# State-space scan on one Trainium2 core: C and B read from a double tile in SBUF, exponent banks in two pairs, instructions 1024 columns wide

## What is computed

```python
dt = jax.nn.softplus(dt_raw + dt_bias)
a = jnp.exp(-jnp.exp(A_log) * dt)
Bh = jnp.repeat(_rms(Braw), HEADS_PER_GROUP, axis=2) + B_bias
Ch = jnp.repeat(_rms(Craw), HEADS_PER_GROUP, axis=2) + C_bias
phi = jnp.cumsum(dt, axis=1)[..., None] * rope_freqs
Bh = _rope(Bh, phi)
Ch = _rope(Ch, phi)
u = xh * dt[..., None]

def step(h, inp):
    a_t, u_t, b_t, c_t = inp
    h = a_t[..., None, None] * h + u_t[..., None] * b_t[:, :, None, :]
    y = jnp.einsum('bhpn,bhn->bhp', h, c_t)
    return (h, y)
```

## Time and profile before

| | us |
|---|---|
| median of 3 runs | 2638.09 |
| lowest and highest | 2632.52 and 2638.44 |
| the profiled execution, its own time | 2641.73 |
| its span, first to last instruction | 2639.7 |
| first product of the scan starts | 203.0 |
| last VectorE multiplication into `M` of the scan starts | 1467.8 |
| VectorE busy between 300 and 1400 us | 96% |

### The profile page before, as it was taken

The page is one execution under the profiler, slowest core; times in us unless marked ns, Lnnn a source line. Parts: engine busy times, 40 slices in busy tenths (PEclk is TensorE's granted clock), DMA queues, the critical chain, the costliest instruction groups (busy, mean ns, idle before and its releaser), DMA issues. The chain is left out here.

```text
span 2639.7 us, 61136 instructions
## 1 busy us (share of the span) xinstructions
PE 2154.0 (82%) x19761; PEld 1590.8 (60%) x19761; DVE 1937.0 (73%) x5279; ACT 1543.8 (58%) x3098; POOL 1486.5 (56%) x2287
## 2 busy tenths in 40 slices
PE   8946888888888888878887799786799767758887
PEld 5634655565655665655655588565355445548887
DVE  4538999999999999999999444466333267747776
ACT  5657898999899999999897122355122112212222
POOL 2447787888788788888787222244111144414444
PEclk9976898988898888998897799888899878879999
DMA  5766666666666666666675367343222233321110
GB/s 171 245 193 175 163 167 174 173 176 174 161 169 180 168 176 175 168 174 175 161 183 142 108 204 233 128 139 124 77 84 84 71 103 116 117 69 37 48 48 28
DMA packets 295374, 373.58 MB, mean 142 GB/s; under 512 B 44852, under 2 KB 234871, under 8 KB 295127
## 3 DMA queue, kind: packets, MB, share of 16 engines
q1 hardware_dynamic: 285254, 343.10, 47.0%
q0 software_dynamic: 9872, 27.28, 3.1%
HBM read 151.03 MB, written 85.00 MB: 89 GB/s over the span
## 5 line engine op out<-in xcount | busy, mean ns | idle before, releaser
L667 POOL TENSOR_TENSOR p_CR<-p_pc 128x256 f32<-128x256 f32 x512 | 373.3, 729 | 189.5 <-DVE p_pc L991 165.9
L671 POOL TENSOR_TENSOR p_BR<-p_pb 128x256 f32<-128x256 f32 x512 | 373.4, 729 | 26.5
L748 PE MATMUL p_ps_sc<-p_CR,p_BR 64*128 64x128 f32 x4096 | 341.6, 313 | 54.8 <-DVE p_M L1004 32.9
L748 PEld LDWEIGHTS p_ps_sc<-p_CR,p_BR 64*128 64x128 f32 x4096 | 289.6, 213 | 113.9 <-issue 86.4
L881 ACT ACTIVATE p_D<-p_ps_x 128x512 f32<-128x512 f32 x512 | 289.5, 593 | 109.5 <-PE p_ps_x L714 108.8
L1004 DVE TENSOR_TENSOR p_M<-p_ps_sc,p_D 128x512 f32<-128x512 f32 x512 | 327.9, 680 | 29.7 <-PE p_ps_sc L748 28.9
L991 DVE SCALAR_TENSOR_TENSOR p_pc<-p_ps_c,p_beta,p_cs 128x256 f32<-128x256 f32 x512 | 243.0, 475 | 46.8 <-DMA p_sn<-p_tr_s 31.3
L763 PE MATMUL p_ps_y<-p_M,p_uexp 128*32 128x128 f32 x4096 | 259.7, 282 | 0.0
L991 DVE SCALAR_TENSOR_TENSOR p_pc<-p_ps_c,p_beta,p_sn 128x256 f32<-128x256 f32 x512 | 242.6, 474 | 0.0
L997 DVE SCALAR_TENSOR_TENSOR p_pb<-p_ps_b,p_beta,p_cs 128x256 f32<-128x256 f32 x512 | 242.5, 474 | 0.0
L997 DVE SCALAR_TENSOR_TENSOR p_pb<-p_ps_b,p_beta,p_sn 128x256 f32<-128x256 f32 x512 | 242.5, 474 | 0.0
(11 more groups left out here) (277 smaller groups left out, 5293.4 us busy)
## 6 DMA issues: line engine op xcount, KB each, us to landing
p_cs<-p_tr_c SPq DMA_DIRECT2D x256, 256.0 KB, 4.1
p_sn<-p_tr_s SPq DMA_DIRECT2D x256, 256.0 KB, 4.5
p_phib<-scratch_phi SPq DMA_DIRECT2D x256, 128.0 KB, 3.1
p_x<-scratch_rt SPq DMA_DIRECT2D x72, 128.0 KB, 2.0
scratch_ro<-p_o POOLq DMA_DIRECT2D x72, 128.0 KB, 2.0
p_xT<-in_xT SPq DMA_DIRECT2D x64, 128.0 KB, 4.6
scratch_u<-p_u SPq DMA_DIRECT2D x16, 512.0 KB, 3.8
scratch_wu<-p_wu SPq DMA_DIRECT2D x16, 512.0 KB, 4.3
```

The costliest lines, as they stand in the source:

```text
L667: e.tensor_tensor(CR[:, p, g, :], pc[:, g % 2, 0, :], pc[:, g % 2, 1, :], ALU.add).then_inc(S["rotC"], 1)
L671: e.tensor_tensor(BR[:, p, g, :], pb[:, g % 2, 0, :], pb[:, g % 2, 1, :], ALU.add).then_inc(S["rotB"], 1)
L748: m = e.matmul(sc_ps[half][:, (g * 2 + b) * L:(g * 2 + b + 1) * L], BR[half * 64:half * 64 + 64, p, 2 * q + g, b * L:(b + 1) * L], CR[half ...
```

## The change

1. `c_ps` and `b_ps` are gone. The tile `bc` in SBUF becomes double (by chunk), and the products read it there. Of the copies into PSUM only the change of sign is left, in place, one ScalarE instruction of 512 columns a chunk (`signed_bc`), one step earlier than `held_bc` was. SyncE's `load_bc` waits for the products of the last chunk but one.
2. The two freed banks make the exponent banks two pairs; the two score banks are now one pair. `exponents` needs one pair free, not both banks.
3. `D`, `M`, the transposes' copies `BT`, the second rounding step of the angles, `magnitude` and `sines` work on twice the columns in half the instructions; of `turned` each half step now has one of eight transposes, where it had two of four, and ScalarE's order is rewritten to that.
4. Four constants of the start are held in tiles that are used later.

The core of the diff:

```diff
-        bc = sb("bc", [P, 4, CT])
+        bc = sb("bc", [P, 2, 4, CT])
...
-        c_ps, b_ps, y_ps, ns_ps = (ps(n) for n in ("c", "b", "y", "ns"))
-        x_ps = [ps(f"x{i}") for i in range(2)]
-        sc_ps = [ps(f"sc{i}") for i in range(2)]
+        y_ps, ns_ps = (ps(n) for n in ("y", "ns"))
+        x_ps = [ps2(f"x{i}") for i in range(2)]
+        sc_ps = ps2("sc")
...
             def load_bc(c):
-                at_least(e, S["bcp_ok"], c, 4, 0)
+                at_least(e, S["prodC"], c, 2 * NG * NB, -2 * NG * NB)
+                at_least(e, S["prodB"], c, 2 * NG * NB, -2 * NG * NB)
...
             def exponents(t, p, q):
-                at_least(e, S["x_ok"], i, 1, 0)
-                bank = [x_ps[(i + half) % 2] for half in range(2)]
+                at_least(e, S["x_ok"], i, 1, -1)
+                bank = [x_ps[i % 2][:, half, :] for half in range(2)]
...
-            def held_bc(c):
+            def signed_bc(c):
                 at_least(e, S["bc_in"], c, 96, 96)
-                for bank, rows, free in ((c_ps, 2, "prodC"), (b_ps, 0, "prodB")):
-                    at_least(e, S[free], c, 2 * NG * NB, 0)
-                    e.activation(bank[:, 0:CT], bc[:, rows, :], ACT.Copy).then_inc(S["bcp_ok"], 1)
-                    e.activation(bank[:, CT:2 * CT], bc[:, rows + 1, :], ACT.Copy, scale=sign[:, :]).then_inc(S["bcp_ok"], 1)
+                e.activation(bc[:, c % 2, 1:4:2, :], bc[:, c % 2, 1:4:2, :], ACT.Copy, scale=sign[:, :]).then_inc(S["bcp_ok"], 1)
...
-                e.activation(D[:, n, :], x_ps[i % 2][:, :], ACT.Exp).then_inc(S["x_ok"], 1)
+                e.activation(D[:, 2 * q:2 * q + 2, :], x_ps[i % 2][:, :, :], ACT.Exp).then_inc(S["x_ok"], 1)
...
-                    e.scalar_tensor_tensor(out=pc[:, g % 2, n - 2, :], in0=c_ps[:, (n - 2) * CT:(n - 1) * CT], scalar=beta[:, k, n, g:g + 1],
+                    e.scalar_tensor_tensor(out=pc[:, g % 2, n - 2, :], in0=bc[:, c % 2, n, :], scalar=beta[:, k, n, g:g + 1],
                                            in1=tr[:, p, g % 2, g // 2, :], op0=ALU.add, op1=ALU.mult).then_inc(S["prodC"], 1)
...
-                    e.scalar_tensor_tensor(out=pb[:, g % 2, n, :], in0=b_ps[:, n * CT:(n + 1) * CT], scalar=beta[:, k, n, g:g + 1],
+                    e.scalar_tensor_tensor(out=pb[:, g % 2, n, :], in0=bc[:, c % 2, n, :], scalar=beta[:, k, n, g:g + 1],
                                            in1=tr[:, p, g % 2, g // 2, :], op0=ALU.add, op1=ALU.mult).then_inc(S["prodB"], 1)
...
-                e.tensor_tensor(M[:, m_slot(p, n), :], sc_ps[n % 2][:, :], D[:, n, :], ALU.mult).then_inc(S["m_ok"], 1)
+                m = m_slot(p, n)
+                e.tensor_tensor(M[:, m:m + 2, :], sc_ps[:, :, :], D[:, n:n + 2, :], ALU.mult).then_inc(S["m_ok"], 2)
```

More of the change, by code:

```diff
@@ L555, in expand @@
                 p = k % 2
-                used, ready = count(e, t, 2 * NG, -2 * NG), count(e, t, 2, 2)
+                used, ready = count(e, t, 2 * NG, -2 * NG), count(e, t, 1, 1)
                 if not (isinstance(t, int) and t < 2):
@@ L568, in load_g @@
                 if t >= 2:
-                    e.wait_ge(S["x_mm"], place["D", t - 2, U - 1] + 1)
+                    e.wait_ge(S["x_mm"], place["D", t - 2, NQ - 1] + 1)
                 for half in range(2):
@@ L787, in new_state @@
             def new_state(t, p):
-                at_least(e, S["x_ok"], place["B", t, NQ - 1], 1, 1)
+                at_least(e, S["x_ok"], place["B", t, 1], 1, 1)
                 at_least(e, wu_got[p], t - p, 8, 16)
@@ L934, in state @@
+                e.activation(BT[:, 2 * h:2 * h + 2, :, :].rearrange("p q a n -> p q (a n)"), x_ps[i % 2][:, :, :], ACT.Copy
+                             ).then_inc(S["x_ok"], 1)
             def state(t):
-                i = place["S", t, 0]
+                i = place["S", t]
                 at_least(e, S["x_mm"], i, 1, 1)
@@ L942, in own, with step @@
                         return bass.AP(tensor=ap.tensor, offset=ap.offset, ap=[list(ap.ap[0]), [2 * P + 16, 2], [32, BATCH * NQ], [1, HD]])
-                    e.activation(own(ST[r, t % NB, 0, 0, h * HD:h * HD + HD]), own(x_ps[i % 2][r, h * HD:h * HD + HD]), ACT.Copy
+                    e.activation(own(ST[r, t % NB, 0, 0, h * HD:h * HD + HD]), own(x_ps[i % 2][r, 0, h * HD:h * HD + HD]), ACT.Copy
                                  ).then_inc(S["x_ok" if h else "kept"], 1)
+            def step(t, k, c):
+                p = k % 2
+                ahead, s3, k3 = t + 3 < T, t + 3, (k + 3) % NB
+                decays(t, 1)
+                if ahead:
+                    in_turns(s3, k3, 0)
+                    near_turns(s3, k3, 0)
+                if t and t <= LAST:
+                    turned(t - 1, 1)
+                if ahead:
+                    in_turns(s3, k3, 1)
+                decays(t, 2)
+                if ahead:
+                    near_turns(s3, k3, 1)
+                    whole_turns(s3, 0)
+                decays(t, 3)
+                if k == 2 and c + 1 < NC:
+                    signed_bc(c + 1)
+                if ahead:
+                    in_turns(s3, k3, 2)
+                    near_turns(s3, k3, 2)
+                if 2 <= t < LAST + 2:
+                    state(t - 2)
+                if t < LAST:
+                    turned(t, 0)
+                if t + 2 < T:
+                    magnitude(t + 2, p)
+                if t + 1 < T:
+                    decays(t + 1, 0)
+                if t + 2 < T:
+                    sines(t + 2, p)
+                if ahead:
+                    in_turns(s3, k3, 3)
+                    near_turns(s3, k3, 3)
+                    whole_turns(s3, 1)
             def all_turns(s):
@@ L952, in _ @@
                 if s == 0:
-                    held_bc(0)
-                for v in range(2):
-                    magnitude(s, s, v)
+                    signed_bc(0)
+                magnitude(s, s)
                 sines(s, s)
-            for n in range(2):
-                decays(0, n)
+            decays(0, 0)
             all_turns(2)
@@ L1010, in new_state @@
                 if t >= NB:
-                    e.wait_ge(S["x_mm"], place["S", t - NB, 0] + 1)
+                    e.wait_ge(S["x_mm"], place["S", t - NB] + 1)
                 for b in range(BATCH):
```

167 lines of the change are left out of this document (56 added, 111 removed).

## The result

The changed kernel takes **2968.04 us** (median of 4 runs, 2966.20 to 2969.22) against 2638.27 us of the kernel before beside it (4 runs, 2632.52 to 2648.45). The ratio is 1.124, with a 95% interval of 1.121 to 1.127: 12.4% slower, 330 us more. The prediction was 2980 us; it is 12 us (0.4%) too high, and the time lies inside its range.

The account below looks back on a forecast made before the run. VectorE was taken to bound the scan, 64 steps of 19.73 us. Meetings 6.5, wider M -0.4 and waits -0.7 gave +5.4 us a step, +345 us on the median 2638.1: 2983, said as 2980 us, range 2870 to 3110.

Parts of the forecast that it names:

- The meetings: Scan: products with two SBUF operands and GpSimd's sums exclude each other; 12 of 0.49 and 2 of 0.31, 6.5 us a step.
- The small term: Scan, first product after M in two quarters of four: waits until `turns` is done, 0.31 us each, two a step.
- the drawing: One quarter of a scan step followed from its first product at 0: three meetings, then `turns` running until 6.21 us.
- The overlap of 0.13 us and the remainder of 0.28 us: Read from another phase: 0.13 us of GpSimd's instruction lies under VectorE's; a blocked 256-column product ends 0.28 us behind GpSimd's.
- Wider M: VectorE's multiplication into M, one of 1024 for two of 512: four a step, -0.4 us (-0.3 to -0.6).
- VectorE's waits: VectorE's idle time for scores, issue and cosine and sine tiles, 0.76 us a step: -0.7 (0 to -0.76).
- The cover named for ScalarE: ScalarE in the scan: even without its spare time, its remaining 16.4 us a step stays below the new step.
- The 128x32 operations of GpSimd: GpSimd's small instructions of 253 ns in the scan: meeting a product gives 0.40, the normal pitch, so they are free.
- A: Rival, scan products: operands don't collide, products keep 475 ns and only gains stay, 2563 to 2612, say 2590 us; chance 0.03.
- B: Rival, scan: all 20 large GpSimd instructions meet products (3195 us), or each meeting costs the whole 0.73 (3175); chance 0.07.
- C: Rival, scan: few meet, eight meetings a step as GpSimd's sums slip under M, +163, 2800 us; chance 0.06.
- D: Rival, scan products: two 32-bit SBUF inputs stream at half rate, +550 on top, 3530 us; chance 0.01.

Follow-up runs that it names:

- e1: Kernel before, with only the products' C and B read from a double SBUF tile, all widths and banks otherwise as before: 2975.61 us, ratio 1.127.
- e2: Kernel before, with B alone read from the SBUF tile and C kept in its PSUM bank: 2828.10 us, ratio 1.072.
- e5: Kernel before, with C alone read from the SBUF tile and B kept in its PSUM bank: 2733.25 us, ratio 1.033.
- e3: Changed kernel with C and B back in two PSUM banks, leaving one pair of exponent banks; wide instructions stay: 2676.94 us, ratio 1.015.
- e6: Changed kernel with GpSimd's two sums replaced by constant fills that read nothing: 2589.05 us, ratio 0.979.
- e7: Changed kernel with the multiplication into M again as two instructions of 512 columns: 2978.27 us, ratio 1.126.
- e4: Kernel before, with only the multiplication into M made 1024 wide and the score banks one pair: 2643.12 us, ratio 1.001.
- e8: Kernel before, with ScalarE's copies of C and B at a chunk's end moved before the step's last two exps: 2665.49 us, ratio 1.000.

## Why the prediction was right, step by step

**The meetings.** Forecast: three of 0.49 us in a quarter and two a step of 0.31 behind `turns`, 6.5 us. Measured: the same three in the same places, each 0.47 to 0.48 above the free 0.47 (0.95, 0.94, 0.94), and two of 0.24 (0.71), together 12 x 0.475 + 2 x 0.24 = 6.2 us. The means over the stretch say it again: (945 - 473) x 8 + (710 - 473) x 8 + (533 - 473) x 8 = 6.15 us. The small term was 0.07 too large: `turns` starts 0.05 us before the end of the sum's record (1011.16, where 1010.48 and 0.73 make 1011.21), and is done that much earlier than in the drawing. e1 shows that this part alone suffices, e2 and e5 that the drawing also tells which operand costs what, e3 and e6 that it vanishes with either side: the VectorE instruction's second SBUF input, or GpSimd's reading.

The overlap of 0.13 us and the remainder of 0.28 us were taken from another phase and other widths; in the scan a product ends 0.28 us (1007.88 after 1007.60) behind the sum. The 0.28 rested on a step that nothing showed beforehand, that a cast of 512 columns with one SBUF input leaves the same remainder as a product of 256 columns with two. That it fits to 0.01 us is in part luck. The Trainium skill's page "SBUF — State Buffer", section "SBUF: two separate sides", lets the loser block for the winner's whole instruction; the trace agrees on who waits for whom, but the two overlap at either end, so that a meeting costs 0.475 us and not the 0.73 of GpSimd's instruction. The same section limits it to a GpSimd operation that reads SBUF; e6 agrees with that, with products of 474 ns beside fills of 312 ns.

**Wider M.** This term was mis-sized: -0.4 us a step forecast, 0.24 by the pitch and 0.12 to 0.16 net (e1 and e7, 8 and 10 us in all), outside its stated range of 0.3 to 0.6. The working took the fixed part of a 512-column instruction as 0.1 us of pitch, between its own bounds of 0.07 and 0.15; it is 0.06, and the term ignored that a shorter M lets the next product run into `turns`.

**VectorE's waits.** Forecast -0.7; they went altogether, 0.76. The sum is 6.15 - 0.24 - 0.76 = +5.15 us a step, measured +5.16, forecast +5.4. The two errors (0.35 us too many for the meetings, 0.1 too much gain) pull in opposite directions and leave 0.24 x 64 = 15 us. That is the distance of the sum's 2983 from 2968; it is 12 from the 2980 that was said, by the rounding alone.

**Off the path.** The cover named for ScalarE held: 939.52/56.25 = 16.7 us a step (16.4 forecast, 18.0 before), with 216.7 us of waiting for TensorE, and TensorE has 395 us to spare. The 128x32 operations of GpSimd are sometimes held up (344 ns for 253) and cost VectorE nothing, as said: the product of 1012.10 runs beside the pair of 1011.85 and keeps its 0.47.

**The rivals.** A (no collision, 2590) falls by products of 945 ns; e6 comes near its price, 2589, where the collision is taken away (GpSimd is also faster there than in rival A). B falls by the count (12 full meetings and 2 small ones a step, not 20) and by 0.475 us for each instead of 0.73. C's two meetings a quarter are e2's pattern, not this kernel's. D (half rate, 3530) falls with every product that meets nobody: 473 ns with two SBUF inputs, 475 with one. The sentence of the Trainium skill named there (Vector Engine (DVE) Microarchitecture Reference, Points that are easy to get wrong) is not borne out by these rows.

**What was wrong outside the prediction's sum.** That work or waiting saved on VectorE in the kernel before is time saved failed twice, in e4 and e8. VectorE was read as the bound by its 96%, and adding to it does cost the full price, less the 0.76 us a step that it had idled. But 18 us less work on it, or 11 us less waiting, bought nothing that the comparison can tell. In e4 the wide M also waits for its second tile (18.9 us for `p_D`), so that run doesn't separate "TensorE and ScalarE are just as near" from "the wide instruction starts later". e8 changes no instruction's width and has its waits come back as waits for scores, which speaks for the first; but its profiled execution also ran at a lower clock, so it is not shown by that alone (see the last section). Which of the two it is stays open.

## What to carry to other kernels

When VectorE and GpSimd work side by side, count each VectorE instruction with two SBUF tensor inputs that would run into a GpSimd instruction that reads SBUF, by drawing one period from the two timelines; a blocked product ended here 0.28 us behind GpSimd's instruction, which made a full meeting 0.475 us, and with one operand in PSUM no product was held up (e3). If only one operand can stay in PSUM, keep the one whose instructions run while GpSimd does: B alone in SBUF cost 186 us (e2), C alone 88 (e5), at the same number of instructions. In this kernel an engine that was 96% busy set the price of what was added to it, but not of what was taken off: before counting a gain on it, ask which engine is next and how near it stands.

## What the runs showed that had not been expected

The time of the kernel before goes with TensorE's granted clock from run to run, and that of e2, in which VectorE waits for nobody, hardly does. Mean clock over the span as a share of full speed, and time:

| Kernel | granted clock | us |
|---|---|---|
| before | 0.892 | 2630.28 |
| before | 0.881 (6 runs) | 2642.43 to 2647.78 |
| before | 0.871 | 2657.08 |
| before | 0.866 | 2664.96 |
| e8 | 0.892 | 2629.84 |
| e8 | 0.882 | 2639.63 |
| e8 | 0.862 | 2656.38 |
| e8 | 0.852 | 2668.71 |
| e2 | 0.877 | 2827.47 |
| e2 | 0.868 | 2829.90 |
| changed kernel | 0.847 to 0.849 | 2966.20 to 2969.22 |
| e7 | 0.847 to 0.852 | 2975.97 to 2980.64 |

A straight line through the 33 runs of the kernel before gives 2646 us at a clock of 0.880 and 14 us for each 0.01, with the runs within some 2 us of it (standard deviation). The same through e8's seven gives 2642 at 0.880, through e4's twelve 2645; e2's four give 3 us for each 0.01. So at equal clock e8 may be worth about 4 us of the 20 hoped for, and e4 about 1; but e8's seven runs had a median clock of 0.862 where those of before had 0.881. Whether the earlier copies bring the lower clock, or those runs had it for another reason, isn't settled; nor does the line itself prove which is cause and which effect. The rows say where the time goes: between the profiled executions of the kernel before and of e8 the scan grew by 34 us (first to last sum into `p_CR`, 1255.5 and 1289.6), while what follows it took 1176.1 and 1169.7 us. And they say how a lower clock could do it: TensorE needs 17.9 instead of 16.7 us a step (e8 above), in a kernel whose VectorE waits for scores. The runs of the changed kernel and of e7 lie too close together (0.847 to 0.852) to show by themselves whether their time follows the clock. Their clock is as low as e8's lowest, but TensorE has room there: it waits 395 us for VectorE.

Second, GpSimd's 128x256 operation that only writes (312 ns) overlaps products with two SBUF inputs without a cost on either side, where its operation that reads costs VectorE 0.475 us.
